# Attention with expert layer on one core: diagonal key tiles between the others, one accumulator bank for the values, a ring of five banks

## What is computed

```python
mod = (silu(c) @ wmod).reshape(1, 6, 1, -1)      # sa, ca, ga, sb, cb, gb
h = layernorm(x) * (1 + ca) + sa
# attention: 16 query heads, 4 key/value heads (groups of 4 query heads), head size 64, rotary, causal
logits = q @ k.T / 8, masked where key > query
x = x + ga * (softmax(logits) @ v @ Wo + bo)
h = layernorm(x) * (1 + cb) + sb
# experts: router picks 2 of 8; each is silu(h @ w1) * (h @ w3) @ w2, weighted
x = x + gb * experts(h)
```

## Time and profile before

| what | us |
|---|---|
| median of 3 runs | 1169.94 |
| lowest, highest | 1166.63, 1174.44 |
| the profiled execution, its own time | 1168.11 |
| its span (first to last instruction) | 1166.6 |
| PE busy, PEld busy | 1086.5, 656.0 |
| DVE, ACT, POOL busy | 851.2, 549.4, 588.1 |
| mean granted clock of PE | 0.979 |

### The profile page before, as it was taken

The page is one execution under the profiler, slowest core; times in us unless marked ns, Lnnn a source line. Parts: engine busy times, 40 slices in busy tenths (PEclk is TensorE's granted clock), DMA queues, the critical chain, the costliest instruction groups (busy, mean ns, idle before and its releaser), DMA issues.

```text
span 1166.6 us, 16696 instructions
## 1 busy us (share of the span) xinstructions
PE 1086.5 (93%) x5727; PEld 656.0 (56%) x5727; DVE 851.2 (73%) x1754; ACT 549.4 (47%) x1155; POOL 588.1 (50%) x633
## 2 busy tenths in 40 slices
PE   3789999999999999999999999999999989888993
PEld 2456565554565555545555655455556455477892
DVE  5777978777778787677888786777787879764333
ACT  2444544545455445454545454544454344653451
POOL 5544655646346557364354673545455624626441
PEclk8899999999999999999999999999999999999997
DMA  8000000000000000000000000000020002332104
GB/s 229 20 1 1 1 1 1 1 1 1 1 1 1 1 1 1 1 1 1 1 1 1 1 1 1 1 1 1 1 72 1 1 1 78 90 82 83 32 24 122
DMA packets 30018, 25.08 MB, mean 22 GB/s; under 512 B 4480, under 2 KB 25344, under 8 KB 29936
## 3 DMA queue, kind: packets, MB, share of 16 engines
q1 hardware_dynamic: 26224, 18.45, 5.8%
q0 software_dynamic: 2272, 4.72, 1.2%
q10 hardware_dynamic: 1440, 0.85, 0.2%
HBM read 15.62 MB, written 8.40 MB: 21 GB/s over the span
## 4 chain that ended last, share of the span: by engine, by line
PE 71%; DVE 13%; issue 6%; POOL 5%; DMA 2%; ACT 1%; ACTq 0%; SPq 0%; DVEq 0%; POOLq 0%
PE PS L1535 18%; PE PS L1483 12%; PE PS L1517 11%; PE PS L1519 9%; PE PS L1619 3%; DVE part_max L1109 3%; PE PS L1458 3%; PE PS L1496 2%; POOL sent L760 2%; PE PS L1585 2%; PE PS L1643 2%; PE PS L1465 2%; PE PS L1559 2%; DVE full L1127 2%; PE PS L1486 1%
## 5 line engine op out<-in xcount | busy, mean ns | idle before, releaser
L1109 DVE TENSOR_REDUCE part_max<-PS 128x1 f32<-128x512 f32 (+2 forms) x576 | 339.7, 618 | 123.2 <-PE PS L1483 100.2
L875 ACT ACTIVATE full<-PS 128x512 f32<-128x512 f32 x384 | 222.7, 599 | 197.8 <-PE PS L1519 186.7
L1517 PE MATMUL PS<-store 128*128 128x512 f32 (+3 forms) x640 | 272.8, 426 | 2.0 <-ACT full L875 1.2
L1483 PE MATMUL PS<-store 128*128 128x512 f32 (+3 forms) x640 | 250.4, 417 | 9.7 <-ACT store L855 4.0
L1519 PE MATMUL PS<-store 128*128 128x512 f32 (+3 forms) x640 | 234.7, 367 | 0.0
L713 POOL TENSOR_TENSOR full<-full 128x512 f32<-128x512 f32 x120 | 155.6, 1328 | 136.9 <-PE PS L1535 135.8
L884 ACT ACTIVATE diag<-PS 128x512 f32<-128x512 f32 (+3 forms) x256 | 111.5, 441 | 207.8 <-PE PS L1522 173.3
L1483 PEld LDWEIGHTS PS<-store 128*128 128x128 f32 x640 | 119.1, 191 | 145.0 <-DVE part_max L1109 62.4
L1535 PE MATMUL PS<-full,V 128*64 128x512 f32 x768 | 190.9, 607 | 0.0
L743 POOL TENSOR_TENSOR lower<-lower 128x320 f32<-128x320 f32 x64 | 60.1, 939 | 255.7 <-DVE lower L1087 253.6
L1517 PEld LDWEIGHTS PS<-store 128*128 128x128 f32 x640 | 123.7, 193 | 72.8 <-ACT diag L884 21.0
(11 more groups left out here) (227 smaller groups left out, 1492.4 us busy)
## 6 DMA issues: line engine op xcount, KB each, us to landing
lower<-in_L_ffn_experts_w_dram SPq DMA_DIRECT2D x16, 256.0 KB, 4.1
sent<-full SPq DMA_DIRECT2D x1, 2574.0 KB, 12.5
full<-sent SPq DMA_DIRECT2D x9, 264.0 KB, 3.9
lower<-made SPq DMA_DIRECT2D x8, 256.0 KB, 5.2
full<-in_L_attn_x_dram SPq DMA_DIRECT2D x2, 512.0 KB, 7.6
out_dram<-XA SPq DMA_DIRECT2D x4, 256.0 KB, 2.7
made<-lower,back_to POOLq DMA_INDIRECT x39, 2.2
wo_sb<-in_L_attn_Wo_dram SPq DMA_DIRECT2D x1, 512.0 KB, 11.1
```

Source lines behind the costliest of these rows:

```text
L875: nc.scalar.activation(full[:, k % QUADS, r, :], PS[:, bank, :], ACT.Exp).then_inc(probs_ready, 1)
L1109: nc.vector.reduce_max(part_max[:, t, b:b + 1], PS[:, bank, 0:width], AX.X).then_inc(ring_dve, 1)
L1483: last = nc.tensor.matmul(PS[:, bank, 0:w], QT(ch % 2, h, t * P, (t + 1) * P), keys[:, 0], start=True, stop=not last_bank)
L1517: nc.tensor.matmul(o, keys[:, 0], QT(ch % 2, h, q0, BANK), start=True, stop=False)
```

## The change

1. **Order of the tiles.** `runs_of` deals the diagonal tiles out between the others. In chunk 3 each four tiles are three from below the diagonal and one diagonal one, in chunk 1 each two are one and one, in chunk 2 one or three and one; chunk 0 has only its diagonal tiles. Tiles come in twos ("runs"); a run's two `pv` steps stand together, after the scores of the next run's first tile. The wait of the first `pv` and the flags `start` and `stop` follow the new order.
2. **Row sums.** `poolsum` and the new `diagadd` (POOL) and `diagsum` (DVE) are steps of one tile each with a semaphore of their own, placed behind the run's `pv`. A diagonal tile is added to the newest sum with its `r` (`diag_into`); in chunk 3 three of four go to POOL, one to DVE, where all four were DVE's. The final `sum` to `norm` steps are placed about a tenth of a pair later.
3. **Values' result.** One accumulator bank (7) in place of two. After a pair's last `pv`, ACT copies it to one of two buffers in SBUF, in turn (`av`, 31 times), and `norm` reads the copy; the next pair's first `pv` waits for the copy. The last pair is read in place.
4. **Ring** of five banks in place of four.
5. **Low part** in one DVE instruction over five heads in place of two; ACT's rounding writes 320 columns in place of 256.
6. Last pair: `rowpart` steps come later, five of eight behind the last `pv`.

```diff
-    SCORE_BANKS, RING_BANKS, KEY_SLOTS = 2, 4, 5
+    SCORE_BANKS, RING_BANKS, KEY_SLOTS = 2, 5, 5
...
+    def runs_of(ch):
+
+        on = [(ch, r) for r in range(TB)]
+        off = [(q, r) for q in range(ch) for r in range(TB)]
+        if ch == 0:
+            return [on[0:2], on[2:4]]
+        runs = []
+        for r in range(TB):
+            ahead = {1: 1, 2: 3 if r % 2 else 1, 3: 3}[ch]
+            tiles, off = off[:ahead], off[ahead:]
+            tiles.append(on[r])
+            runs += [tiles[k:k + 2] for k in range(0, len(tiles), 2)]
+        assert not off
+        return runs
+
+    RUNS = [runs_of(ch) for ch in range(CHUNKS)]
+    ORDER = [[tile for run in runs for tile in run] for runs in RUNS]
+
+    def diag_into(ch, r):
+
+        upto = ORDER[ch][:(ORDER[ch].index((ch, r)) // 2 + 1) * 2]
+        return max([q for q, t in upto if t == r and q < ch], default=0)
+
+    def sums_after(J, run):
+
+        ch = J // PAIRS
+        items = []
+        for q, r in run:
+            if 0 < q < ch:
+                kind = "quadsum" if q == CHUNKS - 2 else "poolsum"
+                items += [(kind, J, m, q, r) for m in range(2)]
+        for q, r in run:
+            if q == ch and ch == 0:
+                items += [("diagadd", J, m, r - 1) for m in range(2) if r % 2]
+            elif q == ch:
+                kind = "diagsum" if diag_into(ch, r) == CHUNKS - 2 else "diagadd"
+                items += [(kind, J, m, r) for m in range(2)]
+        return items
...
+        for run in RUNS[J // PAIRS]:
+            for at, (q, r) in enumerate(run):
                 main += [("s", J, q, r, 0), ("s", J, q, r, 1)]
-                if q < J // PAIRS and r % 2 == 0:
-                    main.append(("gap", 2.1 * len(pending)))
+                if at:
+                    main.append(("gap", 2.1 * at))
                 else:
                     main += pending
-                    pending = []
-                if r == (1 if q < J // PAIRS else 0) and q > 1:
-                    if q < CHUNKS - 1:
-                        main += [("poolsum", J, m, q - 1) for m in range(2)]
-                    else:
-                        main += [("quadsum", J, m, q - 1, part) for m in range(2) for part in range(TB)]
-                pending.append(("pv", J, q, r))
+            pending = [("pv", J, q, r) for q, r in run] + sums_after(J, run)
+        pending.insert(len(run), ("av", J))
...
-      + [place(diag_steps(J), J + 1.02, J + 1.1) for J in range(5)]\
-      + [place(tail_steps(J), J + 1.36, J + 2.02) for J in range(5)]
+      + [place(tail_steps(J), J + 1.46, J + 2.14) for J in range(5)]
...
-    ROWPARTS = {("pv", end - 1, 3, 1): (0, 1), ("pv", end - 1, 3, 2): (2, 3, TB, TB + 1, TB + 2), ("pv", end - 1, 3, 3): (TB + 3,)}
+    ROWPARTS = {("pv", end - 1, 3, 2): (0, TB, TB + 1), ("pv", end - 1, 3, 3): (1, 2, TB + 2, 3, TB + 3)}
...
-    SCORES, RING, AV = 0, 2, 6
+    SCORES, RING, AV = 0, 2, 7
...
+            def values_out(J):
+                ch = local(J)
+                act.wait_ge(pv_done, n.at[("pv", J) + ORDER[ch][-1]] + 1)
+                if J > 1:
+                    act.wait_ge(attn_ready, n.at["norm", J - 2] + 1)
+                nc.scalar.copy(av_sb[J % 2], PS[:, AV, :]).then_inc(av_copied, 1)
...
-                nc.scalar.copy(q_split[:, b, :, 0, :], q)
-                nc.scalar.copy(k_split[:, b, 0, :].rearrange("p (a n) -> p a n", a=2), k).then_inc(parts_ready, 1)
+                nc.scalar.copy(halves_of(b)[:, :, 0, :], rotated[:, b % 2].rearrange("p (h n) -> p h n", n=HEAD))
+                nc.scalar.copy(split[:, b, 2 * QK + 1:2 * QK + 1 + P].rearrange("p (a n) -> p a n", a=2), k).then_inc(parts_ready, 1)
...
-                    nc.vector.tensor_tensor(q_split[:, b, :, 1, :],
-                                            rotated[:, b % 2, 0:QH * HEAD].rearrange("p (h n) -> p h n", n=HEAD),
-                                            q_split[:, b, :, 0, :].bitcast(F32), ALU.subtract)
-                    nc.vector.tensor_tensor(k_split[:, b, 1, 0:HEAD], rotated[:, b % 2, QH * HEAD:QK],
-                                            k_split[:, b, 0, 0:HEAD].bitcast(F32), ALU.subtract).then_inc(low_ready, 1)
+                    nc.vector.tensor_tensor(halves_of(b)[:, :, 1, :], rotated[:, b % 2].rearrange("p (h n) -> p h n", n=HEAD),
+                                            halves_of(b)[:, :, 0, :].bitcast(F32), ALU.subtract).then_inc(low_ready, 1)
...
+                    _, J, m, r = x
                     ch = local(J)
-                    acc = full[:, acc_quad(J, m)]
-                    if part == 0:
-                        dve.wait_ge(probs_ready, n.at["s", J, ch, TB - 1, m] + 1)
-                        dve.wait_ge(quad_added, n.at["quadsum", J, m, ch - 1, TB - 1] + 1)
-                    for r in ((0, 3), (1, 2))[part]:
-                        last = nc.vector.tensor_tensor(acc[:, r, r * P:BANK], acc[:, r, r * P:BANK],
-                                                       diag[:, m, r, r * P:BANK], ALU.add)
-                    if part == 1:
-                        last.then_inc(diag_added, 1)
+                    acc = full[:, acc_quad(J, m), r, r * P:BANK]
+                    dve.wait_ge(probs_ready, n.at["s", J, ch, r, m] + 1)
+                    dve.wait_ge(quad_added, n.at["quadsum", J, m, ch - 1, r] + 1)
+                    nc.vector.tensor_tensor(acc, acc, diag[:, m, r, r * P:BANK], ALU.add).then_inc(diag_added, 1)
...
-                    if q == 0 and r == 0 and J >= 2:
-                        need(attn_ready, n.at["norm", J - 2] + 1)
+                    if (q, r) == ORDER[ch][0]:
+                        if J == 0:
+                            need(gates_taken, 1)
+                        else:
+                            need(av_copied, n.at["av", J - 1] + 1)
```

183 lines of the change are left out of this document (98 added, 85 removed).

## The result

The changed kernel takes 1185.19 us (median of 4 runs, 1181.42 to 1189.03) against 1171.33 for the kernel before beside it: ratio 1.0119, 95% interval 1.0082 to 1.0155. It is slower by some 14 us where I had forecast 13 to 14 less. Timed again in more rounds it stood at 1.0120 (1.0098 to 1.0142). The profiled execution took 1181.42 us, with a span of 1179.6.

A forecast was written before the change was run, and what follows sets the result against it. PE, busy 93% of the span, was taken to bound the kernel by its start-to-start distances. Terms -14.4 + 1.5 - 2 + 1.5 = -13.4 took 1168.1 to 1154.7, 1156.5 against the median, stated as 1156 us; range 1145 to 1172.

The forecast's parts named there:

- The distances, -14.4: PE's row: fewer stretches of values' matmuls, 187 for 246, mean fewer costly changes of kind, taking 14.4 us off.
- nearly all on the path: Claim that the 14.4 us off PE's row would nearly all shorten the kernel, with 1.5 us given back.
- Distances of kind are not saved: Rival: waits of equal size fill what PE's stretches leave; only DVE's 2 us remain, 1166 to 1170; chance 0.18.
- Row sums on POOL, 0 (-2 to +6): 42 more additions on POOL, 40 us, hide in its idle time; 0, from 2 us gained to 6 lost.
- DVE, -2 (0 to -9): DVE loses up to 60 us of 851 busy; 2 us of that reaches PE as gain, range 0 to 9.
- The copy, +1.5 (0 to 28): ACT's 31 copies of the values' result, 0.59 us each, mostly hidden; 1.5 us lost, range 0 to 28.
- No wait of PE names the copy: Sign in the new profile: none of PE's waits names the copy for more than 2 us in total.
- The end, 0 (0 to 2): Five row-sum steps behind the last values, about 3.3 us, hidden by the first fetch; 0 to 2 us lost.
- if pair 30 grows by what the others gain: Sign of being wrong: pair 30, near the end of the attention, lengthens by as much as other pairs gain.
- a group above 238 us: Sign of being wrong: a head group lasts longer than 238 us, where some 236 was forecast against 239.4.
- The slower one: Rival: at 31 exchanges of pairs PE waits 0.6 to 0.9 us for ACT's copy; 1174 to 1183 us; chance 0.10.

The follow-up runs named there:

- the last kernel above: Kernel before with diagonal tiles last in twos, row sums tile by tile and the low part in one instruction; 1.0015 of the kernel before.

## Why the prediction was wrong

**The distances, -14.4: right as a length of PE's row, wrong as a gain.** In the changed kernel PE's usual distances in a middle group add up to 3.5 us less than before, and its busy time fell by 2.8. The step that failed is "nearly all on the path". Waits grew from 8.1 to 11.5 us in the group, which still lasts 239.2. Nor did fewer stretches pay on the whole where the diagonal tiles stay last: with 184 stretches in place of 246, a middle group lasts 236.6 us with copy and ring of five and 237.7 without, against 238.5 for the low part alone, so 0.8 to 1.9 us a group are gained, and nothing in the first group or the last. On the whole the three kernels with diagonal tiles last in twos stand at 0.9968 to 1.0015, none of them below the low part alone at 0.9943; their sums go tile by tile, which was not tried apart. The shorter usual distances speak against the formula by columns alone that the Trainium skill gives for the warm clock ("TensorE: Matmul & The Clock Gate", Back-to-back issue gap), as did the rows; the section gives it for the isolated matmul and says that in a stream the weight loads count too, which my prediction left out.

**What I did not see: how the maxima meet VectorE.** I wrote that side steps move with the main stream, in the rival "Distances of kind are not saved", and stopped there at waits of equal size. They are larger: chunk 1's new order costs 13 us alone, and all the dealing out 17.8. The end of pair 11 was in the trace before, with VectorE 3.5 us behind PE and the turn already 0.71 us late.

**Row sums on POOL, 0 (-2 to +6): 10.3 us.** I priced GpSimd's 42 additions by its own idle time and by the rotations behind them. That left out VectorE, whose instructions lasted longer beside GpSimd's additions. Narrowing these 42 gives 10.3 us back; narrowing all of them gives 17.6 in the new order and 6.2 in the old. The Trainium skill, "GPSIMD Engine Reference", section Specifications, has GpSimd's access to SBUF shared with VectorE, contended where VectorE's instruction has two SBUF inputs. This trace agrees: the norm of 512 columns lasts 673 to 692 ns with one input in PSUM, and 679 to 1772 with both in SBUF. I had the means before, 788 and 726 ns, beside medians of 680 and 682, and did not ask where the difference came from.

**DVE, -2 (0 to -9): too small, though in its range.** The low part alone gives 6.7 us, and 10.4 in the changed kernel. Busy 831 in place of 800 us: the low part came to 771 ns (I took 684), the norms to 1040 in place of 680, the sums to 832 to 861.

**The copy, +1.5 (0 to 28): in its range, but not for its reason.** No wait of PE names the copy, as I had said. Accumulator, copy and ring together cost 4 us in the new order and give 4 with diagonal tiles last. The fifth bank did take the waits for L1109 away from L1483 (2.4 us, none after).

**The end, 0 (0 to 2): 3.6 us.** I took the fetch for the cover. It was no longer last, since the sends and the last sums were both late. Pair 30 grew by 4.8 us (5.9 as the table counts): "if pair 30 grows by what the others gain" and a group above 238 us were the right alarms; both went off.

**The rivals.** No rival held this case. The slower one had ScalarE and the copy; it was VectorE. Its range, 1174 to 1183, is near the result by chance.

**What stays open.** Chunk 2's 3.2 thousandths have no wait that I can name: its groups are the shortest of all (235.9 and 235.7 us) and the loss is at both ends of the kernel. Why kernels with tiles in twos end the first group up to 8 us later, part of it in the opening, was not tried apart. It goes along with PE's clock, whether as cause or as effect of waits in the opening: over the first 130 us the granted clock is 0.95 with the low part alone and 0.93 before, where the first group ends near 288 and 292 us; 0.91 and 0.92 with diagonal tiles last in twos (293 and 294), 0.89 in the changed kernel (297) and 0.88 in the last kernel above (300). My prediction had no term for the clock, and the changed kernel runs at a lower one on the whole, 0.966 in the mean of six executions against 0.976 for the kernel before. How much of the loss passes through it was not tried apart either; that it is not all is shown by the kernel with two accumulators, which keeps 0.978 and still takes 1.0085. How much of GpSimd's cost is VectorE's longer instructions, and how much is GpSimd's own lateness to ScalarE, the narrow additions don't separate, since they shorten both.

## What to carry to other kernels

Before moving work from VectorE to GpSimd, compare the mean of VectorE's two-input instructions with their median: a mean well above it says that GpSimd already stretches them, and GpSimd's idle time says nothing of what new work there will cost VectorE. Where side steps are dealt out by weight, a shorter main row is a gain only if the engine that answers them keeps up: read, for the last step before each hand-over, how far it lags behind the one that feeds it, and how much work covers that. Try each part of a bundle alone; here one instruction in place of two was worth all the gain, and the other parts hid it.

## What the runs showed of the hardware

- VectorE's additions of two SBUF operands at 512 columns (L1197) last 672 to 691 ns with no GpSimd instruction beside them, and up to 1794 beside GpSimd's additions. Reads of PSUM (L1151, a mean of 685 ns before and after) do not change.
- A normalisation with one tensor input, 128 columns, was slowed as well: nine in 4.90 us in place of 2.40. The three beside GpSimd's additions took 1.03 to 1.46 us each, the other six 0.33 to 0.34.
- One wait of PE of 2.4 us in the middle of steady work was followed by 3.4 us at the 1.2 GHz level of its clock (granted 0.53 over 3.5 us), in three groups at the same place; where the wait was absent, as with diagonal tiles last, the granted clock stayed at 1.00. It does not follow each time: in the kernel with chunk 3's diagonal additions narrow the same wait (2.36 us) stands in all three groups, and the clock fell behind two of them. Pairs 11 and 19 last 28.2 and 28.1 us there and pair 27, without the fall, 26.5, so one such fall cost some 1.6 us there, an estimate from this one execution. Its windows behind the waits of pairs 19 and 27:

```profile
615.50:621.00 5.50, 5.50 (x23) 2.96 (x23) 2.44 (x5) 2.67 (x6) 3.50 (x6) 0.69 0.01 3
854.00:859.50 5.50, 5.50 (x32) 2.86 (x30) 3.62 (x7) 3.86 (x9) 4.44 (x8) 1.00 0.00 0
```
